# A bidirectional Mamba block with layer norms on one core: 32 channels of four states in the partitions, dt and dtx replicated through DRAM

## The reference

```
xz = h @ W_in.T                      # x, z: 256 inner channels each
x  = silu(conv4(x) + conv_b)         # causal, depthwise, 4 taps
dt, B, C = split(x @ Wx.T)           # 64 | 16 | 16
dt = softplus(dt @ Wdt.T + bdt)      # [tokens, 256]
A  = -exp(A_log)                     # [256, 16]
for t: s[d,n] = exp(dt[t,d]*A[d,n]) * s[d,n] + dt[t,d]*x[t,d]*B[t,n]
       y[t,d] = sum_n s[d,n] * C[t,n]
y  = (y + x*D) * silu(z);  out = y @ W_out.T
```

## Time and profile before

| | us |
|---|---|
| median of 3 runs (lowest, highest) | 1071.54 (1071.04, 1071.81) |
| the profiled execution, its own time | 1066.46 |
| its span, first to last instruction | 1064.6 |
| busy: DVE / TensorE / POOL / ScalarE | 984.8 / 812.9 / 791.3 / 615.6 |

### The profile page before, as it was taken

One profiled execution on the slowest core, in us unless ns is written; L12 is line 12 of the kernel. 1 busy time (PEld: TensorE's weight loads), 2 busy tenths in 40 slices (PEclk: granted clock), 3 DMA queues, 4 the chain that ended last, 5 costly groups with the idle time before them and its releaser, 6 DMA issues. The chain is left out here.

```text
span 1064.6 us, 8012 instructions
## 1 busy us (share of the span) xinstructions
PE 812.9 (76%) x1964; PEld 345.2 (32%) x1996; DVE 984.8 (93%) x1067; ACT 615.6 (58%) x1006; POOL 791.3 (74%) x353
## 2 busy tenths in 40 slices
PE   6698588879778786878778797888779797767632
PEld 3243233324233232323333242333233242323222
DVE  2889899999999999999999999999999999999946
ACT  3756356665656656566556656665557655653514
POOL 0685788876978787877878787887878787888602
PEclk9899899989989999999999899899999999889976
DMA  3432232234232342323332242323222243322002
GB/s 69 125 98 73 72 113 88 98 78 121 80 83 69 95 114 76 106 87 88 98 96 80 79 116 84 111 82 79 79 90 89 82 120 85 103 86 88 18 0 80
DMA packets 64095, 92.67 MB, mean 87 GB/s; under 512 B 9264, under 2 KB 22576, under 8 KB 64048
## 3 DMA queue, kind: packets, MB, share of 16 engines
q1 hardware_dynamic: 64048, 92.15, 29.4%
HBM read 88.98 MB, written 3.15 MB: 87 GB/s over the span
## 5 line engine op out<-in xcount | busy, mean ns | idle before, releaser
L353 POOL TENSOR_TENSOR dbx<-dtx,b_ring 128x1024 f32<-128x1024 f32 x256 | 612.1, 2406 | 121.3 <-DVE hs L822 86.0
L1059 PE MATMUL y_ps<-ch,ident 128*128 128x512 f32 x1024 | 502.4, 620 | 75.2 <-DVE ch L711 67.1
L549 ACT ACTIVATE da_ps<-dt,neg_a 128x512 f32<-128x512 f32 x512 | 348.9, 688 | 350.6 <-DVE hs L822 348.5
L822 DVE TENSOR_TENSOR_SCAN hs<-da_ps,carry,dbx 128x512 f32<-128x512 f32 x256 | 313.0, 1263 | 13.7 <-ACT da_ps L549 9.4
L822 DVE TENSOR_TENSOR_SCAN hs<-da_ps,dbx 128x512 f32<-128x512 f32 x256 | 297.1, 1202 | 18.3 <-ACT da_ps L549 17.8
L1059 PEld LDWEIGHTS y_ps<-ch,ident 128*128 128x128 f32 x1024 | 195.2, 197 | 312.9 <-issue 198.0
L711 DVE TENSOR_TENSOR ch<-hs,c_ps 128x1024 f32<-128x1024 f32 x192 | 228.8, 1192 | 0.0
L365 POOL TENSOR_TENSOR ch<-hs,c_ring 128x1024 f32<-128x1024 f32 x64 | 151.2, 2363 | 77.6 <-DVE hs L822 76.4
L1017 PE MATMUL pre<-h_t,w_conv 128*128 128x512 f32 x256 | 118.1, 604 | 5.6 <-ACT xs L445 1.6
L1052 PE MATMUL c_ps<-bc_parts,select 128*128 128x512 bf16 x160 | 63.0, 394 | 60.0 <-DVE ch L711 60.0
L1017 PEld LDWEIGHTS pre<-h_t,w_conv 128*128 128x128 f32 x256 | 49.2, 194 | 63.8 <-issue 59.9
(11 more groups left out here) (126 smaller groups left out, 532.7 us busy)
## 6 DMA issues: line engine op xcount, KB each, us to landing
b_ring<-bc_rows SPq DMA_DIRECT2D x256, 256.0 KB, 3.2
c_ring<-bc_rows SPq DMA_DIRECT2D x64, 256.0 KB, 4.3
h_in<-in_L_attn_hidden_states SPq DMA_DIRECT2D x4, 512.0 KB, 4.7
h_res<-in_L_attn_hidden_states SPq DMA_DIRECT2D x4, 512.0 KB, 5.6
out<-hs SPq DMA_DIRECT2D x4, 512.0 KB, 3.2
bc_rows<-x_dbl SPq DMA_DIRECT2D x16, 64.0 KB, 3.0
ch<-in_L_attn_W_in SPq DMA_DIRECT2D x1, 256.0 KB, 4.3
ch<-in_L_attn_W_out SPq DMA_DIRECT2D x1, 128.0 KB, 2.3
```

Source lines behind the costliest of these rows:

```text
L353: nc.gpsimd.tensor_tensor(dbx[:, n % RING], dtx[:, s % 2], b_ring[:, n % RING, :].unsqueeze(1).to_broadcast([P, DT, CHUNK]), ALU.mult).the ...
L549: nc.scalar.activation(da_ps[:, half % DA_BANKS, :], dt[:, s % 2, a, :], ACT.Exp, scale=neg_a[:, g, a, state:state + 1]).then_inc(da_ready, 1)
L822: nc.vector.tensor_tensor_scan(in_scan_order(hs[:, n % RING, a, :], s), in_scan_order(da_ps[:, da_bank(n, a), :], s), in_scan_order(dbx[:, ...
L1059: ins = nc.tensor.matmul(y_ps[:, a, :], ident[:], ch[:, n % RING, a, :], start=False, stop=n == STATES - 1 and s != 1)
```

## The change

The partitions now hold four states (i) of 32 channels (d), partition 32 i + d. A step becomes a unit: 64 channels of four states, as two tiles e = 0, 1 of 32 channels. A group has again 16 units. Unit n belongs to half n // 8 of the channels and to quad (n mod 8) // 2 of the states. The slot r = 0 to 3 names the 64 channels. A B or C tile holds four states, each repeated over 32 partitions, and serves four units; C's broadcast on TensorE is one fp32 matmul for two units. dt and dtx have to be repeated four times over the partitions: they are stored in DRAM (512 KB each a group) and loaded as eight tiles of 32 channels each, four copies a tile. The sum over states is a matmul with four stacked 32x32 identities into one block of 32 output columns, four blocks for two units. `w_scaled` moves into `y_fwd` and `gated`, which are unused at the start.

```diff
-LATER_STAGES = {"copy x_dbl": 0, "rest": 0, "u0": 1, "u1": 2, "take u0": 2, "middle": 3, "third": 3,
-                "take u1": 4, "softplus": 6, "dtx": 9}
+LATER_STAGES = {"copy x_dbl": 0, "u0": 1, "u1": 2, "take u0": 2, "take u1": 4, "softplus": 5, "dtx": 7}
-CLOSING = {"save": 3, "start sum": 3, "gate": 1,
+CLOSING = {"save": 3, "start sum": 3, "gate": 2,
-POOL_C = ((1, 5, 8, 12), (2, 5, 9, 13), (1, 5, 9, 13), (1, 5, 9, 13))
+POOL_C = ((1, 3, 6, 8, 11, 13),) * NG
+def last_of_slot(r):
+    return (r // 2) * (UNITS // DT) + 6 + r % 2
+def last_of_quad(k):
+    return UNITS // DT + 2 * k + 1
...
+            def load_dt(b, s, r):
+                sp.wait_ge(dt_stored, 16 * (group + 1))
+                if group:
+                    sp.wait_ge(da_ready, 2 * (UNITS * (group - 1) + last_of_slot(r) + 1))
+                for e in range(2):
+                    k = BLOCK * (2 * r + e)
+                    sp.dma_start(dt_rep[:, r, e, :], dt_rows[s, k:k + BLOCK, :].partition_broadcast(QUAD)).then_inc(dt_in[r], 16)
+            def load_dtx(b, s, r):      # the same with dtx_stored, dbx_ready, dtx_rep, dtx_rows
+            def load_b(b, s, k):
+                sp.wait_ge(rows_stored, 16 * (group + 1))
+                if group:
+                    sp.wait_ge(dbx_ready, UNITS * (group - 1) + last_of_quad(k) + 1)
+                rows = bc_rows[s, QUAD * k:QUAD * (k + 1), :].unsqueeze(1).to_broadcast([QUAD, BLOCK, CHUNK])
+                sp.dma_start(b_rep[:, k, :], rows).then_inc(b_in[k], 16)
+            def load_c(b, s, k):        # the same, c_rep, waits for ch_pool
             def batch(b, first, last):
                 for s in range(NG):
+                    if group:
+                        load_dt(b, s, 2)
+                        load_dt(b, s, 3)
+                        load_c(b, s, 3)
...                                     # h_in (s = 0) and h_res (s = 2) as before
+                    store_rows(*nxt)
+                    store_dt(*nxt)
+                    load_dt(*nxt, 0)
+                    load_dt(*nxt, 1)
+                    store_dtx(*nxt)
+                    load_b(*nxt, 0)
+                    load_dtx(*nxt, 0)
+                    load_dtx(*nxt, 1)
+                    load_b(*nxt, 1)
+                    load_c(*nxt, 0)
+                    load_b(*nxt, 2)
+                    load_dtx(*nxt, 2)
+                    load_dtx(*nxt, 3)
+                    load_c(*nxt, 1)
+                    load_b(*nxt, 3)
+                    load_c(*nxt, 2)
...
             def times_c(b, s, n):       # GpSimd
+                pool.wait_ge(c_in[k], 16 * (group + 1))
+                pool.wait_ge(scanned, 2 * (UNITS * group + n + 1))
...
-                if stage == "rest":     # and "middle", "third": gone, on DVE and ScalarE
...
+            def replicate_a():          # TensorE, once: A_log to the new layout
...
-                nc.tensor.matmul(c_ps[:, k % C_BANKS, :], select[:, n, :], bc_parts[:, s % 2],
+                nc.tensor.matmul(c_ps[:, n // 2 % C_BANKS, :], select[:, quad_of(n), :], x_dbl[:, s % 2, :],
...
+            def add_units(b, s, n):
+                wait_c_product(pe, b, s, n)
+                wait_c_product(pe, b, s, n + 1)
+                for m in (n, n + 1):
+                    for e in range(2):
+                        ins = nc.tensor.matmul(y_ps[column_block(m, e), half_of(m), :], stack[:], ch[:, m % RING, e, :],
+                                               start=False, stop=quad_of(m) == STATES // QUAD - 1 and s != 1)
+                    ins.then_inc(summed, 1)
```

More of the change, by code:

```diff
@@ L43 @@
 DA_BANKS = 3
-ROWS_AT = 12
-POOL_C = ((1, 5, 8, 12), (2, 5, 9, 13), (1, 5, 9, 13), (1, 5, 9, 13))
-NPC = sum(len(states) for states in POOL_C)
-NVC = NG * STATES - NPC
-C_RING, C_BANKS = 4, 2
+POOL_C = ((1, 3, 6, 8, 11, 13),) * NG
+NPC = sum(len(units) for units in POOL_C)
+NVC = NG * UNITS - NPC
+C_BANKS = 2
 LN1_EPS, LN2_EPS, QUANT_EPS, QB = 1e-5, 1e-3, 1e-5, 128.0
@@ L112, in build @@
         xs = sb("xs", [P, 2, DT, CHUNK])
[L113 to L117, removed]
+        dt = sb("dt", [P, DT, CHUNK])
+        dtx = sb("dtx", [P, DT, CHUNK])
+        x_dbl = sb("x_dbl", [P, 2, CHUNK])
         u = sb("u", [P, DT, CHUNK])
-        b_ring = sb("b_ring", [P, RING, CHUNK])
-        c_ring = sb("c_ring", [P, C_RING, CHUNK])
+        dt_rep = sb("dt_rep", [P, 2 * DT, 2, CHUNK])
+        dtx_rep = sb("dtx_rep", [P, 2 * DT, 2, CHUNK])
+        b_rep = sb("b_rep", [P, STATES // QUAD, CHUNK])
+        c_rep = sb("c_rep", [P, STATES // QUAD, CHUNK])
         dbx = sb("dbx", [P, RING, DT, CHUNK])
@@ L284, in store_rows @@
                 sp.wait_ge(x_dbl_sb, NG * b + s + 1)
-                sp.dma_start(bc_rows[s], x_dbl[0:2 * STATES, :]).then_inc(rows_stored, 16)
-            def load_b(b, s, n):
-                group = NG * b + s
[L290 to L301, removed]
+                sp.dma_start(bc_rows[s], x_dbl[0:2 * STATES, s % 2, :]).then_inc(rows_stored, 16)
@@ L313, in batch @@
                         sp.dma_start(h_res[:], tokens_of(b)).then_inc(h_res_ready, 16)
[L314 to L320, removed]
-            store_rows(0, 0)
+                    if last and s == NG - 1:
+                        return
+                    store_rows(*nxt)
[14 more added lines that the diff above has]
+                    load_c(*nxt, 2)
+            store_rows(0, 0)
+            load_b(0, 0, 0)
+            store_dt(0, 0)
+            load_dt(0, 0, 0)
+            store_dtx(0, 0)
+            load_dtx(0, 0, 0)
+            load_dt(0, 0, 1)
+            load_dtx(0, 0, 1)
+            load_b(0, 0, 1)
+            load_c(0, 0, 0)
+            for k in range(1, STATES // QUAD):
+                load_c(0, 0, k)
+            for k in range(2, STATES // QUAD):
+                load_b(0, 0, k)
+            for r in (2, 3):
+                load_dt(0, 0, r)
+                load_dtx(0, 0, r)
             batches(sp, batch)
@@ L451, in prepare @@
                     act.wait_ge(x_dbl_ps, q + 1)
[L452 to L463, removed]
+                    if q >= 2:
+                        act.wait_ge(u_ps, 2 * (q - 1))
+                        act.wait_ge(rows_stored, 16 * (q - 1))
+                        act.wait_ge(c_ps_ready, UNITS // 2 * (q - 1))
+                    nc.scalar.copy(x_dbl[:, par, :], pre[:]).then_inc(x_dbl_sb, 1)
                 if stage in ("take u0", "take u1"):
@@ L532, in batch @@
                         nc.scalar.preload_act_table_set(EXP)
[L533 to L536, removed]
+                    for n in range(UNITS):
+                        first_half, last_half = 2 * n, 2 * n + 1
                         if n in (FIRST_STAGES["silu"], LATER_STAGES["softplus"]):
@@ L792, in batch @@
                     starts = s in (0, 2)
-                    for n in range(STATES):
+                    for n in range(UNITS):
                         for layer in range(2):
@@ L1117, in batch @@
                 for s in range(NG):
-                    for n in range(STATES):
-                        if n not in POOL_C[s]:
+                    for n in range(UNITS):
+                        if n % 2 == 0:
                             broadcast_c(b, s, n)
@@ L1171, in _ @@
             make_u(0, 0, 1)
+            replicate_a()
             convolve(0, 1, 0, (u_taken, 2))
```

265 lines of the change are left out of this document (149 added, 116 removed).

## The result

| | us |
|---|---|
| before, median of 4 | 1071.67 |
| after, median of 4 (lowest, highest) | 1223.99 (1219.86, 1226.34) |
| ratio after / before | 1.142, 95% interval 1.139 to 1.145 |
| profiled execution of after: own time, span | 1219.86, 1218.0 |

A forecast was written before the change was run, and what follows sets the result against it. DMA confined to four engines was taken as the bound, 73.6 us a group. From 27.9, loads (1075.2), stores, h tiles, rows and silences (42.5), then closing work gave 1285; with 5.1 for the median, 1290 us, range 1150 to 1445.

The forecast's parts named there:

- The loads run on four engines, and that decides: DMA: the [4, 32, 512] loads use four engines, making 73.6 us a group against DVE's 55.0; chance 0.74.
- L = 2.8 us a load: DMA: time of one replicated 256 KB load on four engines, 2.8 us; 384 loads make 1075.2 us.
- The silence, 2.5 us: SyncE waits for dt's store to land before issuing dt loads: 2.5 us each, 17 times, 42.5 us.
- Stores, h tiles, rows: Other DMA transfers: 32 stores 44.8 us, 7 h tiles 11.9 us, rows 3 us.
- The end: After the last C quad lands: POOL's 10 products 23.6 us, DVE's last 2.7, tail 52.3, reaching 1285.
- DVE's sum, -91: VectorE loses bc_rest and bc_parts subtractions and 32 C products: 91.1 us less, 5.7 a group.
- rival A: DMA: new loads spread over all 16 engines, DVE bounds; 1004 us, from 985 to 1030; chance 0.17.
- TensorE, 0: TensorE: state sum -377 to 0, C's fp32 broadcast +50, at worst 863 busy, off the path; taken as 0.
- B (silences that add): DMA: both store round trips add, 7 us of silence twice a group; total near 1475 us; chance 0.05.
- C would have been 28 GB/s an engine: DMA: four engines but at 28 GB/s each, L 2.34, total 1113 us; chance 0.04.
- The signs: Profile: DMA share near 0.25, 90 to 100 GB/s, dt/dtx landings 5 to 12 us, POOL idle over 300, group 73.

The follow-up runs named there:

- e1: The kernel after, with every replicated load (dt, dtx, B, C) cut into four of 32 partitions so that they spread: 1024.49 us, 0.958 of before.
- e4: The kernel before, with B's rows stored in four copies and loaded as [4, 32, 512], on four engines: 1072.89 us, 1.002 of before.
- e3: The kernel after, with the next group's row and dt stores issued after load dt 2 instead of the last C quad: 1187.19 us, 1.110 of before.
- e7: The kernel before, with C broadcast by fp32 matmuls from a double-buffered x_dbl, without the bf16 parts: 1017.62 us, 0.951 of before.
- e12: The kernel after with all loads spread, dtx on GpSimd from the second group on, five C products there: 998.44 us, 0.932 of before.
- e10: The kernel before with C broadcast in fp32, dtx on GpSimd from the second group on, five C products there: 982.30 us, 0.918 of before.
- e2: The kernel after, with only the four B loads of a group cut into four of 32 partitions: 1156.69 us, 1.080 of before.
- e9: The kernel before with C broadcast in fp32, and dtx made by GpSimd instead of VectorE from the second group on: 994.95 us, 0.931 of before.
- e11: The kernel after with all loads spread, and four C products a group on GpSimd instead of six: 1028.18 us, 0.959 of before.
- e8: The kernel before with C broadcast in fp32, and six C products a group on GpSimd instead of four: 1010.87 us, 0.943 of before.

## Why the prediction was right, point by point

- *The loads run on four engines, and that decides.* Right, and shown: in the windows of after (0.26, 102 GB/s), by taking it away (e1), and by putting it into the kernel before (e4). The Trainium skill's rule that a short outermost count confines a DMA to at most that many engines ("DMA: Bandwidth & Descriptors", Rules for kernel authors) agrees with all three.
- *L = 2.8 us a load.* The term that was mis-sized. 102 GB/s over four engines are 25.5 GB/s, 65.5 KB in 2.57 us. I had priced an engine in the best-packed stretch of before, in which all sixteen work; with four active a packet comes every 80 ns or so, not 85 to 91. 384 x 0.23 = 88 us too much. My lower end was 2.5, so the range held it.
- *The silence, 2.5 us.* Gaps over 0.25 us without any packet of 512 bytes or more sum to 32.6 us in the profiled execution, mostly 1.7 to 2.4 behind each store of dt; I had 42.5, 10 us too much. e3 gives 37 back, more than the 19 by which such gaps shrink in its trace (to 13.5); where the other 18 come from is open.
- *Stores, h tiles, rows.* I had 60 us for them. The stream ran from 27.9 to 1133.1 (the last C tile starts GpSimd at 1133.48, where I had 1206.4): 1105.2 less 987 for loads and 32.6 of silence leaves 86. So here 26 us were missing, under 2 a group; which of them is dearer than its bytes was not measured.
- *The end.* From that tile to DVE's last product 32.9 us instead of 26.3 (a small `rstd` operation of 1.0 and two short waits of 1.3 and 1.2 stand between), and 53.5 behind it instead of 52.3. Together -88 - 10 + 26 + 6.6 + 1.2 and -0.7 between the tile's data and its use = -65, as measured: 1285 against 1219.9. So errors of both signs meet in the number: 99 us too much and 34 too little. That it came within 5.4% is in part luck.
- *DVE's sum, -91.* Its busy time fell by 73.3 only (984.8 to 911.5), since dtx, `mv` and the two `bias` rows together grew by 5, 9 and 5 us, here off the path. In rival A's world such rows are on it: e1 measured 1024 against the 1004 that I gave for "spread over all engines", inside its 985 to 1030, near the edge. I had added 1.5 us a group for collisions, but of another kind (a late dbx), and a full DVE with waits inside its rows was not in my list.
- *TensorE, 0.* Right. The sum over states went from 502.4 to 187.9 us busy, and the records are longer than before (814 ns instead of 620), so over four overlap and the column blocks do work side by side:

```profile
L1152 PE MATMUL y_ps<-ch,stack 128*32 128x512 f32 x1024 | 187.9, 814 | 408.3 <-POOL ch L462 329.5
...
L1143 PE MATMUL c_ps<-x_dbl,select 128*128 128x512 f32 x256 | 188.9, 829 | 0.0
```

The fp32 broadcasts cost 188.9 instead of 125, 0.74 us a record at a granted clock of 0.77; in e7, at 0.97, it is 0.53, and the rows that I took 0.49 from were at 0.93. Neither moves the end; e12 beside e10 shows 209 us of TensorE freed for nothing.
- *Rivals.* B (silences that add) was not there: the B load in front of dtx's store covered it, and where it was taken away (e2) about 1 us a group appeared, not 7. C would have been 28 GB/s an engine; it was 25.5, between my 24.05 and that.
- *The signs.* A share at 0.26 and 102 GB/s, POOL waiting 297 us for tiles (over 300 forecast) and a group of 68.8 us (73) came as said. The profile gives no landing for the loads of dt and dtx, so that sign could not be read.

## What to carry to other kernels

Before adding a DMA, look at the outermost count of both access patterns: a broadcast written as `[4, 32, 512]` used four of sixteen engines for the same bytes, and here cutting it into four pieces of 32 partitions turned +14% into -4%. A mean DMA share of 28% can hide engines that never pause: look at short windows for a share that stands still at k/16, and compare the confined engines' work in a period (24 x 2.57 us and the rest) with the period, since below it the shape costs next to nothing. And when work is moved from a full engine to another that can hold it up, as GpSimd does VectorE here, look at the mean duration of the first engine's small rows, not only at its busy sum.

## What the runs showed that was not expected

- An issue on SyncE takes 0.33 us when the engines have room and 2.5 us when the four engines are behind; it then runs at their pace.
- The step from bf16 parts to an fp32 broadcast, the plainest part of the change, is worth 52.5 us alone (e7), and the move of dtx to GpSimd another 23 (e9), while 38 us of C products moved off VectorE were worth 4 to 7 (e11 to e1, e7 to e8, each with overlapping intervals), and 19 us of them 13 once dtx was gone from VectorE (e9 to e10, one product a group).
- A VectorE addition over 128x4 elements took 0.17 us before and 1.07 in the mean in e1, beside a fuller GpSimd.
